# An adaLN block with attention and a mixture of experts on one core: operand rows loaded in another order, first batch normalized on VectorE, expert tiles turned four ahead, tail in pieces

## What is computed

```python
sa, ca, ga, sb, cb, gb = split(silu(c) @ wmod)        # six rows for each batch
h = layernorm(x) * (1 + ca) + sa
q, k, v = h @ Wq.T (16 heads of 8), h @ Wk.T (8), h @ Wv.T (8)     # K and V shared by all heads
x = x + ga * (softmax(q k^T / sqrt(8)) v)
h = layernorm(x) * (1 + cb) + sb
top 2 of 8 experts by router; expert e: gelu(h @ w1[e].T + b1[e]) @ w2[e].T + b2[e]
x = x + gb * (sum of the two experts' outputs, weighted by a softmax of the two logits)
```

## Time and profile before

| | us |
|---|---|
| median of 3 runs (lowest, highest) | 681.35 (680.12, 682.44) |
| profiled execution, its own time | 684.1 |
| its span, first to last instruction | 682.0 |
| PE busy in the span | 590.1 (87%) |
| DVE, ACT, POOL busy | 500.7, 450.3, 374.0 |
| mean granted TensorE clock | 0.954 of full |

### The profile page before, as it was taken

The page is one execution under the profiler, slowest core; times in us unless marked ns, Lnnn a source line. Parts: engine busy times, 40 slices in busy tenths (PEclk is TensorE's granted clock), DMA queues, the critical chain, the costliest instruction groups (busy, mean ns, idle before and its releaser), DMA issues.

```text
span 682.0 us, 19386 instructions
## 1 busy us (share of the span) xinstructions
PE 590.1 (87%) x6826; PEld 331.1 (49%) x6826; DVE 500.7 (73%) x1125; ACT 450.3 (66%) x795; POOL 374.0 (55%) x616
## 2 busy tenths in 40 slices
PE   1694979999999999999999999997699997699970
PEld 1341223433343343443443443431698997699960
DVE  5477787989879879789789889781367667656862
ACT  1283257887878878878778788787445654456751
POOL 3995101114347666665756757667244774656782
PEclk9996998999999999999999999997789999799995
DMA  8644030020020120120211210002121321236414
GB/s 221 232 141 163 26 125 7 11 70 31 11 88 18 40 83 17 54 70 19 63 57 27 63 52 26 23 16 60 49 76 55 80 83 55 62 92 199 148 56 143
DMA packets 46646, 49.65 MB, mean 73 GB/s; under 512 B 10920, under 2 KB 40856, under 8 KB 45816
## 3 DMA queue, kind: packets, MB, share of 16 engines
q1 hardware_dynamic: 37848, 36.94, 18.2%
q0 software_dynamic: 4544, 9.38, 4.1%
q10 hardware_dynamic: 4160, 2.10, 1.2%
HBM read 30.30 MB, written 17.47 MB: 70 GB/s over the span
## 4 chain that ended last, share of the span: by engine, by line
PE 62%; DVE 14%; issue 6%; ACT 6%; DMA 5%; POOL 3%; SPq 2%; DVEq 0%; POOLq 0%; ACTq 0%
PE ps L884 13%; PE ps L843 11%; PE ps L952 10%; DVE neg_max L1180 10%; PE ps L874 10%; PE ps L963 9%; DMA V<-v_cols 2%; ACT P L1049 2%; DMA Q<-max_parts 2%; ACT diag L1059 2%; PE ps L943 1%; PE ps L911 1%; PE ps L926 1%; PE ps L862 1%; POOL P L293 1%
## 5 line engine op out<-in xcount | busy, mean ns | idle before, releaser
L1180 DVE TENSOR_REDUCE neg_max<-ps 128x1 f32<-128x512 f32 x512 | 321.5, 683 | 64.8 <-PE ps L843 63.5
L1049 ACT ACTIVATE P<-ps,zero 128x1024 f32<-128x1024 f32 x256 | 272.3, 1111 | 76.1 <-PE ps L874 75.3
L843 PE MATMUL ps<-K,Q 128*32 128x512 bf16 x2048 | 185.6, 387 | 12.5 <-DMA V<-v_cols 9.8
L874 PE MATMUL ps<-Q,K 128*32 128x512 bf16 x2048 | 157.6, 385 | 13.7 <-ACT P L1049 9.7
L1105 ACT ACTIVATE parts<-ps,parts 128x128 f32<-128x128 f32 x312 | 89.2, 370 | 79.9 <-PE ps L952 79.8
L884 PE MATMUL ps<-P,V 128*32 128x512 f32 x1024 | 135.5, 604 | 0.1
L1321 POOL DMA_INDIRECT y_rows<-P,to_now x78 | 86.0, 1102 | 71.4 <-DVE to_now L1216 55.0
L843 PEld LDWEIGHTS ps<-K,Q 128*32 128x32 bf16 x2048 | 54.6, 96 | 117.4 <-DVE neg_max L1180 55.7
L952 PE MATMUL ps<-parts 128*128 128x128 f32 x624 | 87.2, 285 | 14.4 <-issue 14.4
L874 PEld LDWEIGHTS ps<-Q,K 128*32 128x32 bf16 x2048 | 51.6, 97 | 86.8 <-issue 26.5
L952 PEld LDWEIGHTS ps<-parts 128*128 128x128 f32 x624 | 79.8, 200 | 17.3 <-issue 17.3
(11 more groups left out here) (190 smaller groups left out, 528.1 us busy)
## 6 DMA issues: line engine op xcount, KB each, us to landing
Q<-q_parts SPq DMA_DIRECT2D x24, 384.0 KB
xs<-h_sorted SPq DMA_DIRECT2D x78, 65.0 KB
W<-w_t SPq DMA_DIRECT2D x2, 2048.0 KB, 11.0
Q<-y_rows SPq DMA_DIRECT2D x8, 512.0 KB, 4.9
q_parts<-parts SPq DMA_DIRECT2D x8, 384.0 KB
X<-x ACTq DMA_DIRECT2D x4, 512.0 KB, 8.3
diag<-att_u SPq DMA_DIRECT2D x128, 16.0 KB
out<-Q SPq DMA_DIRECT2D x8, 256.0 KB, 2.6
```

The lines of the kernel that those rows point to most:

```text
L843: ins = eng.matmul(ring_bank(*unit)[QUAD * q:QUAD * (q + 1), :], Q[buffer_of(g)][:, g % NG * G + j, at:at + QUAD], K[buffer_of(g)][:, 0, : ...
L874: ins = eng.matmul(bank(2 * u + j)[QUAD * q:QUAD * (q + 1), :], K[p][:, 1, at:at + QUAD], Q[p][:, g % NG * G + 2 * u + j, :], start=True, ...
L1049: nc.scalar.activation(P[s % 2][:, 2 * u:2 * u + 2, :], bank(2 * u, 2).rearrange("p (j t) -> p j t", j=2), ACT.Exp, bias=zero[:], scale=SC ...
L1180: eng.tensor_reduce(neg_max[g % 2][:, j * T + s:j * T + s + 1], ring_bank("maximum", g, s, j), AX.X, ALU.max, negate=True).then_inc(ring_u ...
```

## The change

1. **Operand rows.** Copies of one Q row stand in neighbouring partitions (row outermost, copy inside); K's parts are stored in the order that fits. The same bytes move, with the same number of DMAs.
2. **Front.** EARLIER is the first 8 tiles, LATER the other 24. DVE normalizes batch 0, POOL batches 1 to 7. The upper half of x is loaded from SP's queue. Q[0] is cleared after `silu_done`; `diag` is built after all batches are split (`lo_done`). ACT's first modulation waits for one of POOL's six steps instead of six.
3. **Routes.** `route(5, 0)` and `(5, 1)` stand right behind `slots(5)` in group 29, `(5, 2)` and `(5, 3)` in group 30, instead of one in group 30 and three in 31. Variance, root and rows of batch 6 leave the loop.
4. **Tiles.** Rows are turned four tiles ahead instead of two, `up` two ahead instead of one, weights four instead of three, with five weight and hidden buffers instead of four. The extra work has new places; `number_tiles` is in two parts, `fill` waits for the first step only.
5. **Combination.** `mix` gates a batch in one instruction instead of four. Batches 6 and 7 are loaded, mixed, summed and stored in eight pieces of 128 tokens; SP issues the loads and stores of one batch, ACT those of the other. Two of the three stores left go ahead of the loads.

```diff
-                eng.dma_start(Q[p][at:at + 3 * DK, :, :].rearrange("p h t -> p (h t)"),
-                              q_parts[bass.ds(b, 1), blk, :, :, :].rearrange("a d h t -> d (a h t)").partition_broadcast(3)
+                eng.dma_start(Q[p][rows, :, :].rearrange("p h t -> p (h t)"),
+                              q_parts[b, blk].rearrange("d h t -> d (h t)")[:, None, :].to_broadcast([DK, 3, NH * S])
...
-        EARLIER, LATER = slice(0, NT // 2), slice(NT // 2, NT)
+        EARLIER, LATER = slice(0, NT // XC), slice(NT // XC, NT)
...
-            for operand in (rw, K[0], K[1], Q[0]):
+            for operand in (rw, K[0], K[1]):
                 eng.memset(operand[:].bitcast(I32), 0).then_inc(op_set, 1)
+            eng.wait_ge(silu_done, START + 1)
+            eng.memset(Q[0][:].bitcast(I32), 0).then_inc(op_set, 1)
...
             eng.wait_ge(loaded, START + LOADED)
+            eng.wait_ge(lo_done, START + 2 * B)
             for b in range(0, B, 2):
...
+                if half == 0:
+                    eng.wait_ge(var_done, START + 8)
+                    normalize(eng, 0, first_xn)
...
-        XD, YD, HD, UD = 8, 16, 4, 3
+        XD, YD, HD, UD = 8, 16, 5, 3
...
-        AHEAD = 3
+        AHEAD, TURNS, UPS = 4, 4, 2
...
+                    if batch_at(g, 5) == CHUNK[0] - 1:
+                        route(eng, CHUNK[0] - 1, 0)
+                        route(eng, CHUNK[0] - 1, 1)
                     if batch_at(g, 1) is not None:
                         add_attention(eng, batch_at(g, 1))
...
-                    for t in range(T):
-                        eng.wait_ge(mix_own, START + b * MIX_OPS + t + 1)
-                        eng.tensor_tensor(res[p][:, t, :], res[p][:, t, :], mod_row[:, b, GB, :], ALU.mult).then_inc(mix_own, 1)
+                    eng.wait_ge(mix_own, START + mix_ops(b) + T)
+                    eng.tensor_tensor(res[p], res[p], mod_row[:, b, None, GB, :].to_broadcast([128, T, D]), ALU.mult).then_inc(mix_own, 1)
...
+        def late_loads(eng, b):
+
+            for p in [(NTILES + k) % YD for k in range(YD)]:
+                eng.wait_ge(scattered[p], 16 * tiles_at(p, YD, NTILES))
+            eng.wait_ge(mix_own, START + mix_ops(b - CD + 1))
+            for t in range(T):
+                at = b * 2 * S + t * 2 * 128
+                eng.dma_start(y[b % CD][:, t, :, :], y_rows[at:at + 2 * 128, :].rearrange("(p n) d -> p n d", n=2)
+                              ).then_inc(late_loaded[(b - CHUNK[0]) * T + t], 16)
```

More of the change, by code:

```diff
@@ L182, in _ @@
                 rows = x.rearrange("b (t p) d -> p (b t) d", p=128)
-                for c, arrived in enumerate(x_arrived):
+                for c in range(XC // 2):
                     these = slice(c * NT // XC, (c + 1) * NT // XC)
-                    eng.dma_start(X[:, these, :], rows[:, these, :]).then_inc(arrived, 16)
+                    eng.dma_start(X[:, these, :], rows[:, these, :]).then_inc(x_arrived[c], 16)
             @block.vector
@@ L501, in adaln_block @@
         out_stored = [sem(f"out_stored{p}") for p in range(CD)]
+        PIECES = CHUNK[1] * T
+        late_loaded = [sem(f"late_loaded{n}") for n in range(PIECES)]
         LAST = B - 1
@@ L687, in route, with count_tiles @@
                                        hs[p][:, t, :], None).then_inc(routed[p], 16)
-        def number_tiles(eng, c):
+        def count_tiles(eng, c):
             own = Chain(eng, meta_own, c * META_OPS)
-            n, at, most = TILES[c], c * TILES[0], CHUNK[c] * T
-            of_tile, these = [128, n, E], slice(at, at + n)
+            most = CHUNK[c] * T
             end = runs[c][:, most, :]
             eng.wait_ge(slot_own, START + slot_ops(sum(CHUNK[:c + 1])))
-            number, ge = line[:, 0:n], passed_e[:, 0:n, :]
+            own.link(eng.tensor_copy(fill_at[:, c, :], end[0:1, :]))
             if c == 0:
@@ L1003, in _ @@
                 eng.wait_ge(ring_used, START + len(USED_AT))
-                eng.wait_ge(ring_copied, START + COPIED_AT["rows turned", LAST - 1])
+                eng.wait_ge(ring_copied, START + COPIED_AT["sums turned", LAST])
                 eng.wait_ge(meta_own, START + META_OPS)
-                turn_rows(0)
-                turn_rows(1)
-                up(0)
+                for t in range(TURNS):
+                    turn_rows(t)
+                for t in range(UPS):
+                    up(t)
                 for t in range(NTILES):
-                    if t + 2 < NTILES:
-                        turn_rows(t + 2)
-                    if t + 1 < NTILES:
-                        up(t + 1)
+                    if t + TURNS < NTILES:
+                        turn_rows(t + TURNS)
+                    if t + UPS < NTILES:
+                        up(t + UPS)
                     if t == 0:
@@ L1139, in _ @@
                                 maxima_out(g + 1)
[L1140 removed]
+                            if s == 0 and u == 1 and batch_at(g, 3) in IN_LOOP:
                                 normalize_rows(batch_at(g, 3), (0, 1))
[L1142 removed]
+                            if s == 1 and u == 0 and batch_at(g, 3) in IN_LOOP:
                                 normalize_rows(batch_at(g, 3), (2, 3))
@@ L1172, in _ @@
                         first_rows(COMBINE_AT[t])
-                for b in range(CHUNK[0], B):
-                    first_rows(b)
+                late_loads(eng, LAST)
+                for n in range(PIECES):
+                    b, t, p = late_place(n)
+                    eng.wait_ge(late_loaded[n], START + 16)
+                    nc.scalar.activation(first[p][:, t, :], y[p][:, t, 0, :], ACT.Copy,
+                                         scale=weight[:, b * T + t, 0:1]).then_inc(first_done, 1)
+                for n in range(T, PIECES):
+                    late_store(eng, n)
             @block.vector
@@ L1302, in _ @@
                         mix(COMBINE_AT[t])
-                for b in range(CHUNK[0], B):
-                    mix(b)
+                late_weigh(0)
+                for n in range(1, PIECES):
+                    late_weigh(n)
+                    late_gate(n - 1)
+                late_gate(PIECES - 1)
             @block.gpsimd
```

248 lines of the change are left out of this document (148 added, 100 removed).

## The result

| | before | changed kernel |
|---|---|---|
| median of 4 runs, us | 681.45 (680.12 to 682.44) | 661.72 (658.49 to 668.61) |
| ratio, 95% interval | | 0.9696 (0.9635 to 0.9756) |
| profiled execution, own time and span | 684.1, 682.0 | 658.49, 656.6 |

The changed kernel is 3.0% faster. The forecast was 646.9, range 638 to 660: the direction held, and the time fell 14.8 us above the forecast, beyond the range. The median counts all four executions, also a disturbed one of 668.61 that the ratio leaves out; the other three have 659.22 as theirs. On two other chips the changed kernel took 659.86 and 661.38 (kernel before 682.52 and 683.03).

A forecast was written before the change was run, and what follows sets the result against it. PE was taken as the bound where it has work, with time lost at seams and in tile-stage stops. Gains 9.3 + 6.1 + 0.6 + 14.5 + 4.0 = 34.5 from the median 681.35 gave 646.9, range 638 to 660.

The forecast's parts named there:

- The front: Up to the first row maximum: 9.3 us gained, bounds 3.7 and 11.
- The four things counted: Front: L371 freed of the clearing, clearing delaying variances instead, DVE freed of `diag`, batch 0's operands ready before DVE.
- Start of attention: PE's waits for `shift` and the next load, and half clock behind: 6.1 us gained, bounds 0 and 6.7.
- Passage: From attention to the tiles: 0.6 us gained, bounds a loss of 2 and a gain of 4.
- Tiles: Tile stage: look-ahead covers PE's stops behind DVE's extra work, 14.5 us gained, bounds 7 and 20.
- The 0.9 for the last tile: Tile stage's end: 0.9 us gained from a stop of PE at the last tile.
- Tail: Batches 6 and 7 in pieces: last store issued at 673.3, 4.0 us gained, bounds 1 and 6.
- Three engines: Rival: Q's copies stay on three DMA engines, 11.7 us given back, 658.6; chance 0.10.
- SP's queue binds the tile loop: Rival: turned rows find tiles not loaded, tile stage gains 7 instead of 14.5, 654.4; chance 0.14.
- All covers hold: Rival: tile stage gains 19, passage 4, tail 5, giving 638; chance 0.08.
- Slower: Rival: the new row order puts a whole load on one DMA engine, about 790; chance 0.03.
- no change: Rival: every gain at a seam is given back at the next; chance 0.03.

The follow-up runs named there:

- e8: Changed kernel without the new wait (`lo_done`) ahead of building `diag` on POOL: 696.46 us, ratio 0.9758 to the kernel before.
- e1: Kernel before with only the new order of Q's rows and of K's parts that follow: 704.30 us, ratio 0.9855.
- e14: Changed kernel with the split of group 31 ahead of `add_attention(6)` on POOL: 656.50 us, ratio 0.9622 to the kernel before.
- e15: Changed kernel with all route scatters of batch 5 behind the split of group 31: 658.06 us, ratio 0.9626 to the kernel before.
- e9: Changed kernel repeated unchanged in session 2: 659.86 us (kernel before 682.52), ratio 0.9674.
- e17: Changed kernel repeated unchanged in session 4: 661.38 us (kernel before 683.03), ratio 0.9678.
- e6: Changed kernel with less look-ahead, rows turned two tiles ahead and first product one: 666.08 us, ratio 0.9764 to the kernel before.
- e3: Changed kernel with the old tail, batches 6 and 7 loaded, mixed and stored whole: 693.73 us, ratio 0.9707 to the kernel before.
- e5: Changed kernel with the last eight additions on DVE instead of POOL: 656.88 us, ratio 0.9645 to the kernel before.
- e7: Changed kernel with each store one tile later in SP's queue: 658.59 us, ratio 0.9661 to the kernel before.

## Why the prediction was right in part, and where it was wrong

**The front: right (9.9 for 9.3).** The four things counted came as described: L371's neighbour free of the clearing, the clearing holding one instruction of the variances instead, DVE no longer met by `diag` (shown by e8), the operands no longer last (e1). One figure in it was wrong without effect: I had the load of batch 0 over at 48, from 8 engines at the packet rate of three; it ended behind 54. In the packets of the trace 7.3 rows of 16 KB are under way on average (2.9 before), close to the eight counted, but each takes about 1.0 us (0.6 before), and the 72 rows take 10 us where 5.3 stood in the forecast. DVE was ready 0.8 us after it, so nothing was left of the margin. The share of 0.46 in a load is near what the count of engines gave, 8 of 16. The Trainium skill, "DMA: Bandwidth & Descriptors", "Why a DMA increments its semaphore by 16 and not by 1", gives 8 engines for this shape; the trace agrees in the number, and the rate of 127 GB/s is not 8/3 of 83.

**Start of attention: right (15.7 ahead at group 5, 15.4 forecast).** `shift` is not waited for in group 1, and no half clock falls there. e1 shows that the order of the rows does it alone.

**Passage: the late group 31 was seen, its price was mis-sized.** The stop is 3.52 for 3.4 forecast, and the reason holds, with one thing added: it takes the scatters and `add_attention(6)` together (e14 and e15 each move one of them, and the stop is gone). What failed is the sum behind it: "0.6, bounds a loss of 2 and a gain of 4". The loss was 2.0. The term that was too small is the delay of the fill: on the time scale of the kernel before (15.9 added) it starts at 465.3, where I had 463.4, and the tile loads at 479.9, where I had 477.5. The routes' earlier end can't pay for it: the last scatter ends at 452.3 in the changed kernel and at 451.9 in e14, while the tile loads start at 463.96 and 460.10, so the end of the routes is not what they wait for. They wait for SP's own steps behind `shift`, and each microsecond by which `shift` is late passes to the first tile: 4.1 earlier in e14 than in e17, and 4.1 earlier at `up(0)`. The passage has 13.7 us of half clock in the profiles of both kernels; the changed kernel has 10.2 in e9 and 13.7 in e17, and e14, without the stop, 10.2, so what the stop adds to it can't be told. The look-ahead's own price there, four turns 1.1 us apart instead of two, 2.2 us, was in the forecast within "stays at 483".

**Tiles: right in the mechanism, 2.6 too much.** The stage gained 13.2 up to tile 77's first product, and e6 shows that none of it is left without the look-ahead. The long stops behind DVE fell from 4.57 and 2.13 to at most 0.9, and the loads of tiles 70, 73 and 76 cost 3.5 us for 3.7 forecast. The 0.9 for the last tile turned into a loss of 1.2: the scatter of tile 77 starts 3.8 us after the start of its last product instead of 2.5. DVE's mix of batch 5 stands between the results of tiles 76 and 77 in both kernels; what sets the end now is POOL, which works off the sum of batch 4 and the scatters of tiles 75, 76 and 77 from 633.78 on without a wait for PE or DVE, and starts the last 1.0 us after its rows are ready (636.9). In sum 11.9 for 14.5.

**Tail: the step that failed (a loss of 0.5 for a gain of 4.0).** I followed the last store: "the last store is issued at 673.3: 4.0". Two things were missing. First, the pieces queue: they land 642.7 to 646.8, the late ones 4 us behind the first, and from 646.2 on DVE needs 0.7 us for each of six, with POOL behind it. From the last landing to the last store's issue it is 5.2 us; I had 2.0, for one piece alone. My lower bound of 1 named this queue and still took a gain. So even the last store's issue did not move: 14.1 us behind the start of tile 77's scatter, before 13.7. POOL's last addition ends 13.6 us behind that start, before it was 13.3. Second, the last store does not set the end: POOL's DRAIN ends 4.8 us after its last addition and 2.9 after SP's last wait. It was to be seen in the profile of before, where the last store had landed at 679.4 and the span ended at 682.0; I had not asked what filled these 2.6 us. e3 shows the new tail worth nothing, e5 shows 2.3 us of the stretch (3.0 in the medians) to be had by giving POOL nothing to do there.

**The rest of the miss** is the median: I subtracted a difference between two single executions from a median, and had no term for where the second execution would lie in its own spread. The four executions of the result lie 10.1 us apart.

**The rivals.** Three engines: refuted (0.46, e1). SP's queue binds the tile loop: no more than the 3.5 us counted; e7 recovers 1.3 at most. All covers hold: no. Slower and no change: no.

## What to carry to other kernels

Look at what ends the span before working on what ends the work: an engine's closing drain counts from its last instruction, so the last short steps belong on an engine whose drain is short, and a shorter store chain beside a longer drain gives nothing. When a step on a queue is moved ahead of another, follow the moved one's first waiter, and then what stands in that waiter's own queue; it paid here to put the small step that others wait for first. And a forecast made from one profiled execution needs the spread of single executions in its range on both sides.

## What was not expected of the hardware

- POOL's closing DRAIN ended 4.7 to 4.8 us behind its last instruction (677.06 to 681.73, 651.53 to 656.37) and 4.8 behind in e5 too, where that was the addition of batch 5 (641.4 to 646.2). DVE's took 0.4 to 0.8 us, ACT's 0.15 to 1.2, PE's 0.7 to 0.8. What makes POOL's so long was not measured.
- With 7.3 row copies of 16 KB in flight each took about 1.0 us, with 2.9 in flight 0.6 to 0.7: 2.2 times the DMA share, 1.5 times the rate.
- A chip can be 4.5% slower with the same code and clock (mean granted clock 0.957 for 0.963 of the changed kernel), through stops of PE and ACT that name no releaser, in the last groups of attention and in the tile loop.
